# One-unit cross attentions of a fused transformer kernel: reordering VectorE, ScalarE and GpSimd within a turn

## What is computed

```python
def _L0_xattn_ref(q, k, v, Wq, bq, Wk, bk, Wv, bv, Wo, bo):
    B, LQ, _ = q.shape
    LKV = k.shape[1]
    qh = (q @ Wq + bq).reshape(B, LQ, HEADS, D_K).transpose(0, 2, 1, 3)
    kh = (k @ Wk + bk).reshape(B, LKV, HEADS, D_K).transpose(0, 2, 1, 3)
    vh = (v @ Wv + bv).reshape(B, LKV, HEADS, D_K).transpose(0, 2, 1, 3)
    scores = jnp.einsum('bhqd,bhkd->bhqk', qh, kh) * scale
    attn = jax.nn.softmax(scores, axis=-1)
    out = jnp.einsum('bhqk,bhkd->bhqd', attn, vh)
    concat = out.transpose(0, 2, 1, 3).reshape(B, LQ, D_MODEL)
    return concat @ Wo + bo
...
x = x + _L0_xattn_ref(_layernorm(x, axis=-1), ctx_512, ctx_512, ...)
```

## Time and profile before

| | us |
|---|---|
| median of 3 runs | 2466.41 |
| lowest and highest run | 2459.04, 2468.11 |
| profiled execution | 2461.6 |
| its span | 2459.8 |
| VectorE busy, whole span | 1813.6 (74%) |
| TensorE busy (matmul) | 2128.7 (87%) |
| ScalarE busy | 1335.6 (54%) |
| GpSimd busy | 1248.3 (51%) |

### The profile page before, as it was taken

One profiled execution on the slowest core, in us unless ns is written; L12 is line 12 of the kernel. 1 busy time (PEld: TensorE's weight loads), 2 busy tenths in 40 slices (PEclk: granted clock), 3 DMA queues, 4 the chain that ended last, 5 costly groups with the idle time before them and its releaser, 6 DMA issues. The chain is left out here.

```text
span 2459.8 us, 67263 instructions
## 1 busy us (share of the span) xinstructions
PE 2128.7 (87%) x22352; PEld 1624.6 (66%) x22352; DVE 1813.6 (74%) x4599; ACT 1335.6 (54%) x2823; POOL 1248.3 (51%) x1940
## 2 busy tenths in 40 slices
PE   6869997999988779599999997899888999998866
PEld 4558995555656568566666666666667888886533
DVE  6975554666659766489999977688698866666987
ACT  3435552344335456355555556455476888884457
POOL 5547625555535367477777745333174334333433
PEclk9969998999999969899999999899999999999988
DMA  8032211000000223200000000000000311210000
GB/s 330 1 116 80 76 52 30 15 13 14 11 2 1 84 73 105 66 14 11 10 10 10 9 2 21 10 1 0 19 2 5 92 58 59 64 48 24 0 8 28
DMA packets 82432, 96.69 MB, mean 39 GB/s; under 512 B 16736, under 2 KB 61665, under 8 KB 80161
## 3 DMA queue, kind: packets, MB, share of 16 engines
q1 hardware_dynamic: 74016, 77.12, 9.8%
q0 software_dynamic: 8192, 16.79, 2.3%
HBM read 56.51 MB, written 37.36 MB: 38 GB/s over the span
## 5 line engine op out<-in xcount | busy, mean ns | idle before, releaser
L1729 DVE TENSOR_TENSOR l2f_h_lo<-l2f_h,l2f_h_hi 128x512 fp32r<-128x512 f32 x256 | 187.4, 764 | 100.9 <-ACT l2f_h_hi L1650 100.8
L1019 POOL TENSOR_TENSOR a_pm<-a_pt,tri_post 128x256 f32<-128x256 f32 x256 | 179.7, 732 | 73.1 <-ACT a_pt L673 72.7
L1657 ACT ACTIVATE l2f_h<-l2f_f,ahead 128x512 f32<-128x512 f32 x256 | 174.5, 689 | 49.5 <-DVE l2f_h_lo L1729 32.3
L815 DVE TENSOR_REDUCE l1s_negm<-l1s_s 128x6 bf16<-128x768 f32 x128 | 123.1, 962 | 95.3 <-PE l1s_s L490 95.2
L1824 POOL TENSOR_TENSOR l2f_acc<-l2f_tmp,l2f_acc 128x512 f32<-128x512 f32 x56 | 73.1, 1306 | 207.1 <-DVE l2f_tmp L1747 207.1
L673 ACT ACTIVATE l1s_pt<-l1s_st 128x768 f32<-128x768 f32 x128 | 96.9, 812 | 145.0 <-PE l1s_st L528 145.0
L815 DVE TENSOR_REDUCE a_negm<-a_s 128x4 bf16<-128x1024 f32 x128 | 156.2, 1220 | 24.6 <-PE a_s L490 24.5
L1650 ACT ACTIVATE l2f_h_hi<-l2f_h 128x512 fp32r<-128x512 f32 x256 | 154.5, 633 | 0.0
L673 ACT ACTIVATE a_pt<-a_st 128x1024 f32<-128x1024 f32 x128 | 126.3, 1062 | 2.6 <-PE a_st L528 2.6
L689 ACT ACTIVATE a_q_hi<-a_pa 128x256 bf16<-128x256 f32 x64 | 24.6, 384 | 185.7 <-PE a_pa L456 185.7
L1541 PE MATMUL l2f_f<-l2f_x_hi,l2f_w_hi 128*128 128x512 f32 x256 | 101.8, 398 | 1.2 <-POOL l2f_w_lo L1811 1.2
(11 more groups left out here) (573 smaller groups left out, 6914.5 us busy)
## 6 DMA issues: line engine op xcount, KB each, us to landing
expert_rows<-zeros SPq DMA_DIRECT2D x16, 1056.0 KB, 17.4
l2f_wrow<-weights_by_expert SPq DMA_DIRECT2D x64, 256.0 KB, 3.2
l0f_w<-in_l0f_w SPq DMA_DIRECT2D x8, 640.0 KB, 9.7
l0f_x_in_sb<-expert_rows SPq DMA_DIRECT2D x72, 64.0 KB
expert_rows<-l0f_y SPq DMA_DIRECT2D x72, 64.0 KB, 1.6
l1f_x_in_sb<-expert_rows SPq DMA_DIRECT2D x72, 64.0 KB
expert_rows<-l1f_y SPq DMA_DIRECT2D x72, 64.0 KB, 1.9
ahead<-in_l2f_w SPq DMA_DIRECT2D x6, 512.0 KB, 4.6
```

Of the source, the lines that this page charges most:

```text
L815: dve.tensor_reduce(dst, src, AX.X, ALU.max, negate=True).then_inc(max_done, 1)
L1019: last = pool.tensor_tensor(pm[:, par, heads_, kt, :], pt[:, par, heads_, kt * (T + P):kt * (T + P) + P], K["tri_post"][:].unsqueeze(1).br ...
L1657: act.activation(h[:, j], psum_f[j][:], ACT.Gelu, bias=col(e, j)).then_inc(h_ready, 1)
L1729: dve.tensor_tensor(h_lo[:, pos % 2, j], h[:, j], h_hi[:, pos % 2, j].bitcast(F32), ALU.subtract)\
```

## The change

Four calls are moved, for `U == 1` alone. On ScalarE the token copy `turned` goes between the two exponentials. On VectorE the loop over `plan` becomes the function `norms_of`, called behind the residual and the second maximum; it is called ahead of them still where `U == 4`. On GpSimd `keys` goes from the end of the turn to behind `context`, ahead of `lay_values`, the roots and the preset. No instruction is added or taken away, and the three phases have no `merge` in their plan.

```diff
--- before.py
+++ after.py
@@ -720,10 +720,13 @@
                 n2, b2, u2, pos2 = at(2)
                 if inside(n):
                     exps(n, pos, 0)
+                if U == 1 and inside(n2):
+                    turned(b2)
+                if inside(n):
                     exps(n, pos, 1)
                 if U == 4 and inside(nn) and (per_unit or un == 0):
                     copy_v(nn, bn, un, posn)
-                if inside(n2) and u2 == 0:
+                if U == 4 and inside(n2) and u2 == 0:
                     turned(b2)
                 if inside(n2) and (per_unit or u2 == 0):
                     copy_qk(n2, b2, u2, pos2)
@@ -871,6 +874,17 @@
                     dve.tensor_tensor(dst, rden[:, 1, :], add_t[:, bass.ds(b * T, T)], ALU.add)\
                        .then_inc(norm_done, 1)
 
+            def norms_of(at, kinds):
+                for when, what, i in sorted(plan, key=lambda p: (-p[0], p[2])):
+                    na, ba, ua, posa = at(LEAD - when)
+                    if inside(na) and ua == 0 and what in kinds:
+                        if what == "merge":
+                            merge_choice(ba, (posa // U) % 2, i)
+                        elif what == "stats":
+                            ln_stats(ba, i)
+                        else:
+                            ln_apply(ba, i)
+
             def residuals(b):
                 dve.wait_ge(w_done, b + 1)
                 view = psum_act[:, 0:T].rearrange("p (t d) -> p t d", t=TT)
@@ -890,13 +904,8 @@
                 nn, bn, un, posn = at(1)
                 if inside(nn):
                     maxima(nn, posn, 0)
-                for when, what, i in sorted(plan, key=lambda p: (-p[0], p[2])):
-                    na, ba, ua, posa = at(LEAD - when)
-                    if inside(na) and ua == 0:
-                        if what == "merge":
-                            merge_choice(ba, (posa // U) % 2, i)
-                        elif what != "gather":
-                            ln_stats(ba, i) if what == "stats" else ln_apply(ba, i)
+                if U == 4:
+                    norms_of(at, ("merge", "stats", "apply"))
                 residual_now = inside(nw) and uw == U - 1 and store_t is None
                 if residual_now and inside(nn):
                     residuals(bw)
@@ -904,6 +913,8 @@
                     maxima(nn, posn, 1)
                     if before:
                         join_maxima(nn, posn)
+                if U == 1:
+                    norms_of(at, ("stats", "apply"))
                 if paired and U == 1 and inside(n1):
                     turn_sums(n1, n1)
                     divide(n1)
@@ -1029,6 +1040,7 @@
                     mask(n, pos, 1)
                 if U == 1 and inside(n2):
                     context(b2, pos2)
+                    keys(n2, b2, u2, pos2)
                 if not per_unit and inside(nn) and un == 0:
                     lay_values(bn, posn)
                 for when, what, i in sorted(plan, key=lambda p: (-p[0], p[2])):
@@ -1042,7 +1054,7 @@
                             gain(ba, i)
                 if bob is not None and inside(nn) and un == 0:
                     preset(bn)
-                if not per_unit and inside(n2):
+                if U == 4 and not per_unit and inside(n2):
                     keys(n2, b2, u2, pos2)
 
             run(pool, emit)
```

## The result

The changed kernel takes 2511.91 us (median of 4 runs, 2508.38 to 2514.59), the kernel before, beside it, 2463.59. The ratio is 1.0195, interval 1.0178 to 1.0212: slower by 48 us. The forecast was slower, 2495 with a range up to 2508, so the direction holds and the size is 17 us short, 4 us outside the range.

What follows compares the result with a forecast made beforehand. The prediction took the closed round through four engines, lengthened by `v_f`'s wait for `vb`, as deciding: 10.0 + 10.4 + 12.9 us less 3 gave +30 on 2461.6, 2496 on the median's scale, stated as 2495, range 2472 to 2508.

Steps and rivals of the forecast that it cites:

- The token copy and the residual off the round: TensorE's waits for `xq_t` and the residual disappear: 0.36 and 0.19 us per turn gone from the round.
- The round through `vb`: ScalarE's `v_f` waits for `vb`, now behind GpSimd's keys: +1.25 us, `l0` round 7.46; chance 0.78 (2480 to 2508).
- the sum: 15 turns per stage: `l0` 10.0, `l1c` 10.4, `l3` 12.9, together 33.3 us, less 3 for overlapped seams: +30.
- The upper bound of 2508: Top of the range; the bound above +30 was a round of 7.7 us, +43, if each hand-over is 0.08 dearer.
- The seam rival: `vb` comes in time and VectorE sets the pace at 6.83 + 0.35 per turn: +16 us, 2482; chance 0.10.
- the seam's price: VectorE stands still between its two maxima, waiting for the second scores: 0.3 to 0.35 us per unit.
- The freed port: VectorE's `on_t` multiplies move away from GpSimd's keys, VectorE stays the bound: 0.41 per unit, -18 us, 2448; chance 0.06.
- The contention that the prediction booked at 0: VectorE's second `on_t` multiply runs beside GpSimd's key products; moving it could save 0 to 0.4 us per unit.
- VectorE's busy share at about 86%: Sign in the profile after: VectorE's busy share down to some 86%, idle ahead of the second and first maxima.
- Norms behind the second maximum cost nothing: On VectorE the norms land ahead of the sums; their reader, the turn of the tokens, is a step away: nothing.

Runs made afterwards that it cites:

- values-first kernel: The changed kernel with the value layout ahead of the keys on GpSimd, the keys still ahead of the roots: 2442.66 us, 0.991 of the kernel before.
- late token copy: The values-first kernel with the token copy behind both exponentials again: 2479.44 us, 0.9968 of the kernel before.
- old VectorE order: The values-first kernel with the norms between VectorE's two maxima again: 2480.04 us, 0.9977 of the kernel before.
- two value buffers: The changed kernel, keys first, with a second `v_f`, so the copy waits for the `vb` of a turn earlier: 2472.93 us, 0.9955 of the kernel before.
- two kernels with late keys: Kernel before with only VectorE's norms moved behind the second maximum: 2504.39 us, 1.0158; changed kernel with keys back at the end of GpSimd's turn: 2528.02 us, 1.0166.

## Why the prediction was right in direction and short in size

- **The token copy and the residual off the round**: right. Both waits are gone after. That the second exponential, 0.35 later, harms nothing holds too (token copy alone, 0.997).
- **The round through `vb`**: right, and shown from both ends. From `k_f`'s start to `v_f`'s end it takes 101.64 to 104.02, 2.38 us, forecast 2.47; the turn 7.36, forecast 7.46. Remove the cause by order or by a buffer, and the ratio goes from 1.0195 to 0.991 or 0.9955. In `l1c` full-clock turns are 7.7 to 8.0 (forecast 7.7 to 7.9), in `l3` 7.2 to 7.4 (7.47). One small slip is in the sum: the rows give 6.28 of work, and with the two waits of 0.36 and 0.19 that is the whole turn of 6.83, so the 0.07 taken off to get 6.21 stands in no row.
- **The step that failed: the sum took every TensorE duration at the granted clock of 1.00.** The prediction read this clock in the earlier trace rows, used durations taken at it, and never asked whether it would be granted still when the wait for `v_f` goes from 0.5 to 1.7 us a turn. The missing term is 21 us: 51.4 us of stage length after, 30.5 with TensorE kept busy in the same wait. TensorE's busy time, 22 us longer in the changed kernel for the same work, fits that. With that term the forecast would have been 2516. The upper bound of 2508 held only dearer hand-overs.
- **The seam rival (+16)**: VectorE does wait before its second maxima, 0.67 us and more for the output projection in the rows after. But this is inside the longer round. With the wait for `vb` gone VectorE's order earns 14 us, so the seam's price, booked at 0.3 to 0.35 a unit, doesn't show as a loss. With half of the norms put into the seam the later turns get 0.1 us shorter each, which is what these runs show of its price.
- **The freed port (-18)**: wrong for this change, right as a mechanism. Its condition was that `v_f` is held back by less than 0.6 us, and here it was 1.0 to 1.4. The values-first kernel meets the condition and lands at -21 in stage length, but that is not the port alone: the token copy is in it too, and 4 us are first turns. The contention that the prediction booked at 0 exists: 0.25 us a unit less on the multiplies in the changed kernel itself, where it gains nothing, and 0.42 in the values-first kernel, against 0.3 measured for the order as a whole. The seam's 0.1 would fit the difference; that it is the difference was not tried.
- **VectorE's busy share at about 86%**: it was 74% of the stretch in `l0` (14.77 of 20). With TensorE kept busy, so at full clock and with turns of about the forecast length, it is 81% (16.14 of 20), so the clock makes part of the difference, and the shorter multiplies part of the rest.
- **Norms behind the second maximum cost nothing**: true only while the keys stand ahead of the roots. With the keys last it costs 1.6%, by the keys' wait for the roots that the prediction didn't look for.
- The two gains don't add: late token copy +17.4, old VectorE order +14.4, together 31.8, while values first is only 21.1 below the kernel before (in the later turns 12.2 and 11.4, together 23.6, against 17.2). Each counts fully only when the other bound is gone as well.

## What to carry to other kernels

When a change lengthens a wait of TensorE, ask first whether its clock will still be granted; the lengthening of the round itself is then only a part of the price (30 of 51 us here). When an instruction is moved ahead in a queue, look for what it now stands before: the keys had to pass the roots but not the values, and a single buffer behind the values closed the round. Between such alternatives it is the same few instructions in another order that make 1.0195 or 0.991.

## What the runs showed of the hardware

- The granted clock falls behind waits of this size: with waits of TensorE of 1.7 us in turns of 7.4 us it goes to 0.50 in about every fourth turn of `l0` and every second of `l1c` (113 to 117 us in the rows shown), while TensorE is busy again. It falls too with VectorE's order alone, where TensorE's longest waits are 1.6 us (0.86 from 80 to 100 us). In the kernel before, with waits of 0.52, 0.36 and 0.19 us in a turn of 6.8, it was 1.00 in the stretches shown. With the 1.7 cut to 0.5 by matmuls without use it was 1.00 again from the third turn of every stage on. Why one turn falls and the next doesn't, and whether the one long wait or all the idle time together counts, these runs don't tell apart; `l3`, with a like wait, gave back only 2.4 us; the long second turn of that stage stays, and these runs don't explain it.
- A VectorE multiply of 128x128 fp32 with two SBUF inputs takes 288 ns in the kernel where no large GpSimd product falls beside it (GpSimd's roots over 128x2 do run beside it there, and cost it nothing), and on average 497 to 550 in those where products of 128x256 do. GpSimd's `vb` grows as well: a median of 0.45 us in the values-first kernel, 0.52 with two value buffers, where it meets the multiplies.
- Of three chips one ran the kernel before 0.9% faster than the two others (2464 against 2487 and 2486 us). The unchanged stretch between `l1c` and `l3` makes most of it: 1408 to 1412 against 1428 to 1431 us. The stages themselves agree: 354.9 and 355.5 us in the two kernels with late keys, one on each chip.
